# Attend and feed-forward parts of a Performer block as one program: the crossing between them written out per engine

## The reference

```
out = x + attn(xn) + ffn(xn)

attn:  q,k,v = xn @ wq, wk, wv              (reshaped to B=4, S=2048; 16 heads of 32)
       phi(u) = exp(u@omega.T - |u|^2/2 - max) / sqrt(128) + 1e-6     (128 features)
       kv = sum_s phi(k) v ;  z = sum_s phi(k)
       a  = (phi(q) @ kv) / (phi(q) @ z) @ wo
       x1 = layernorm(xn + a)
       x2 = layernorm(x1 + gelu(x1 @ w1 + b1) @ w2 + b2)      (512 -> 2048 -> 512)
ffn:   xr, xk = mixes of xn and the row before it
       r  = sigmoid(xr @ W_r.T) * (relu(xk @ W_k.T)^2 @ W_v.T)
```

## Time and profile before

| | us |
|---|---|
| median of 3 runs | 3691.76 (3691.68 to 3693.3) |
| profiled execution | 3692.05 |
| its span in the trace | 3690.2 |
| PE busy | 3544.2 |
| DVE / ACT / POOL busy | 2070.7 / 1839.5 / 1394.2 |

### The profile page before, as it was taken

The page is one execution under the profiler, slowest core; times in us unless marked ns, Lnnn a source line. Parts: engine busy times, 40 slices in busy tenths (PEclk is TensorE's granted clock), DMA queues, the critical chain, the costliest instruction groups (busy, mean ns, idle before and its releaser), DMA issues. The chain is left out here.

```text
span 3690.2 us, 71667 instructions
## 1 busy us (share of the span) xinstructions
PE 3544.2 (96%) x27762; PEld 3105.4 (84%) x27762; DVE 2070.7 (56%) x3304; ACT 1839.5 (50%) x3976; POOL 1394.2 (38%) x957
## 2 busy tenths in 40 slices
PE   7999999999699999999999949999999999999998
PEld 6888888887588888888888849988889989888887
DVE  5877777777567777777777633333333333333332
ACT  5777777777456656565665633333333323333332
POOL 2554545454244545454454412222222222222222
PEclk9999999999799999999999979999999999999999
DMA  2222222221223232232323241111111111111111
GB/s 104 87 78 70 90 78 73 73 88 54 95 81 102 82 97 91 88 97 88 102 84 98 83 129 68 46 44 43 45 44 46 45 38 46 44 43 45 45 45 46
DMA packets 151680, 262.70 MB, mean 71 GB/s; under 512 B 23184, under 2 KB 44176, under 8 KB 151440
## 3 DMA queue, kind: packets, MB, share of 16 engines
q1 hardware_dynamic: 151440, 259.46, 20.9%
HBM read 155.48 MB, written 103.94 MB: 70 GB/s over the span
## 5 line engine op out<-in xcount | busy, mean ns | idle before, releaser
L1484 DVE TENSOR_TENSOR ffn_hT_lo<-ffn_hid,ffn_hT_hi 128x512 fp32r<-128x512 f32 x256 | 334.3, 1334 | 489.4 <-ACT ffn_hT_hi L1460 489.4
L97 PE MATMUL ffn_hidden<-ffn_yT_hi,ffn_wa_hi 128*128 128x256 f32 x2048 | 573.3, 280 | 11.8 <-DVE ffn_yT_lo L1480 11.8
L97 PE MATMUL ffn_hidden<-ffn_yT_hi,ffn_wa_lo 128*128 128x256 f32 x2048 | 573.3, 280 | 0.0
L97 PE MATMUL ffn_hidden<-ffn_yT_lo,ffn_wa_hi 128*128 128x256 f32 x2048 | 572.3, 279 | 0.0
L1451 ACT ACTIVATE ffn_hid<-ffn_hidden,ffn_bias 128x256 f32<-128x256 f32 x512 | 213.2, 467 | 669.6 <-PE ffn_hidden L97 650.8
L233 POOL TENSOR_TENSOR ffn_n_rstd<-ffn_n_base,ffn_n_power 128x2 f32<-128x2 f32 x32 | 22.4, 700 | 1073.7 <-DVE ffn_n_negmean L228 1073.7
L97 PE MATMUL ffn_result<-ffn_wb_hi,ffn_hT_hi 128*128 128x512 f32 x1024 | 412.2, 403 | 2.6 <-DVE ffn_hT_lo L1484 2.6
L97 PE MATMUL ffn_result<-ffn_wb_hi,ffn_hT_lo 128*128 128x512 f32 x1024 | 404.5, 395 | 0.0
L97 PE MATMUL ffn_result<-ffn_wb_lo,ffn_hT_hi 128*128 128x512 f32 x1024 | 404.2, 395 | 0.0
L97 PEld LDWEIGHTS ffn_hidden<-ffn_yT_hi,ffn_wa_hi 128*128 128x128 f32 x2048 | 384.5, 188 | 20.8 <-DVE ffn_yT_lo L1480 12.1
L97 PEld LDWEIGHTS ffn_hidden<-ffn_yT_lo,ffn_wa_hi 128*128 128x128 f32 x2048 | 385.0, 188 | 8.8
(11 more groups left out here) (238 smaller groups left out, 9876.8 us busy)
## 6 DMA issues: line engine op xcount, KB each, us to landing
attend_uq<-u_d SPq DMA_DIRECT2D x33, 512.0 KB, 4.6
ffn_y_in<-y_d SPq DMA_DIRECT2D x33, 512.0 KB, 3.6
keys_xin<-in_L_attn_x_dram SPq DMA_DIRECT2D x32, 512.0 KB, 5.3
xn_d<-keys_xn SPq DMA_DIRECT2D x32, 512.0 KB, 4.2
xT_d<-keys_xT_whole SPq DMA_DIRECT2D x32, 512.0 KB, 2.6
u_d<-keys_uq SPq DMA_DIRECT2D x32, 512.0 KB, 2.8
attend_xTf<-xT_d SPq DMA_DIRECT2D x32, 512.0 KB, 5.1
r_d<-attend_gate SPq DMA_DIRECT2D x32, 512.0 KB, 3.2
```

The source lines that it names most:

```text
L97: last = pe.matmul(out, stationary[a], moving[b], start=start and n == 0, stop=stop and n == len(TERMS) - 1)
L1484: dve.tensor_tensor(hT[n % HB].lo[:, :, :], hid[n % 2][:, :, :], f32(hT[n % HB].hi[:, :, :]), ALU.subtract).then_inc(h_ready[n % HB], 1)
```

## The change

Attend and feed-forward become one Block, with no barrier between them and one end for both.

- Tiles get addresses by hand. The attend tiles are laid out in a table. Most feed-forward tiles lie over attend tiles: the weights, cut in eight pairs each (wa0 to wa7, wb0 to wb7), over attend weights and buffers that die at different times; stages s, x_in, r_in over diff, mixed, xTf; y_in over uq; hT over ka, act_k2 and gate. PSUM banks are shared: result 0 is turn, hidden 0 to 3 are feat 0 to 3, result 1 is num, turn 0 and 1 are gated 0 and 1.
- In place of the barrier stand waits on attend's semaphores (`left`) at the first use of each place.
- The last attend group (-1 in the lists), the tails of the two before it, and feed-forward group 0 are one list per engine (`..._CROSSING`). On PE, after num 3 of the last group: turn, w1 0 to 2, w2 0 and 1, w1 3, then the last two wo, then the rest of group 0.
- Groups 1 to 31 of feed-forward are written out in Python, the hardware loop is gone. The loads of a group that doesn't exist (the old `after`) are gone, and so is the second identity.

```diff
+FFN_OVER = (("wa0_hi", "wk_hi", 0), ("wa0_lo", "wk_hi", 4096), ("wb0_hi", "wk_hi", 8192), ("wb0_lo", "wk_hi", 12288),
+            ("wa1_hi", "wr_hi", 0), ("wa1_lo", "wr_hi", 4096), ("wb1_hi", "wr_hi", 8192), ("wb1_lo", "wr_hi", 12288),
...
         def run(eng, do):
-            do("weights", 0, 0)
-            do("weights", 1, 0)
-            do("turn", 0, 0)
-            for job, n, lead in BODY:
-                if job == "w1" and n + 2 < NH:
-                    do("weights", n + 2, 0)
-                if job != "base":
-                    do(job, n, lead)
-                if job == "w1" and n == NH - 1:
-                    do("base", 0, 0)
-            with eng.Fori(1, G - 1) as g:
+            for g in range(1, G):
                 for job, n, lead in BODY:
-                    do(job, n, g + lead)
-            for job, n, lead in BODY:
-                if lead == 0:
-                    do(job, n, G - 1)
-
-        block = ctx.enter_context(nc.Block())
-
-        @block.sync
-        def _(sp):
-            sp.dma_start(y[:, :, :], y_g[0]).then_inc(y_loaded, 16)
-
+                    if g + lead < G:
+                        do(job, n, g + lead)
+
+        def room(n):
+
+            return ((left.k_full, G), (left.r_full, G), (left.r_full, G), (left.out_full, G), (left.num_full, NC * G),
+                    (left.num_full, NC * G), (left.wo_full, G), (left.wo_full, G))[n]
...
+                if job == "y" and g == 0:
+                    sp.wait_ge(left.q_turned, 2 * G)
+                    sp.wait_ge(left.squared, TG * G)
+                    sp.wait_ge(left.y_stored, 16)
+                    sp.dma_start(y[:, :, :], y_g[0]).then_inc(y_loaded, 16)
                 if job == "weights":
+                    if n == 0:
+                        sp.wait_ge(left.mix_full, 2 * G)
+                        sp.wait_ge(left.mix_ready, 2 * G)
+                        sp.wait_ge(left.carried, G + 1)
                     for k in (2 * n, 2 * n + 1):
                         wait(sp, w_split, k - ns + 1)
                         sp.dma_start(stage(k), pieces[k][0]).then_inc(loaded[k % ns], 16)
...
-                    sp.dma_start(y[:, :, :], y_g[after(g, G)]).then_inc(y_loaded, 16)
+                    if isinstance(g, int) and g == 0:
+                        sp.wait_ge(left.y_stored, 16 * G)
+                        sp.wait_ge(left.r_stored, 16 * G)
+                    if not (isinstance(g, int) and g == G - 1):
+                        sp.dma_start(y[:, :, :], y_g[g + 1]).then_inc(y_loaded, 16)
...
+                    if isinstance(g, int) and g == 0:
+                        pool.wait_ge(consts_loaded, 16 * 4)
+                        pool.wait_ge(left.sq_ready, TG * G)
+                        pool.wait_ge(left.feat_full[HC - 1], 4 * G)
...
+                    act.wait_ge(*room(n))
+                    if n == NH - 1:
+                        act.wait_ge(left.o_ready, 2 * G)
...
+                        if isinstance(g, int) and g < 2:
+                            pe.wait_ge(left.wo_free[m], G - 1 + g)
+                            pe.wait_ge(left.out_free[m], G)
...
+PE_CROSSING = (("attend", "max", 0, -1), ("attend", "num", 3, -2), ("attend", "k", 0, -1), ("attend", "max", 1, -1),
+               ("attend", "k", 1, -1), ("attend", "r", 0, -1), ("attend", "below", 0, -1), ("attend", "feat", 0, -1),
+               ("attend", "r", 1, -1), ("attend", "out", 0, -1), ("attend", "num", 0, -1), ("attend", "out", 1, -1),
+               ("attend", "feat", 1, -1), ("attend", "num", 1, -1), ("attend", "wo", 0, -2), ("attend", "num", 2, -1),
+               ("attend", "wo", 1, -2), ("attend", "num", 3, -1), ("ffn", "turn", 0, 0), ("ffn", "w1", 0, 0),
+               ("ffn", "w1", 1, 0), ("ffn", "w1", 2, 0), ("ffn", "w2", 0, 0), ("ffn", "w2", 1, 0),
+               ("ffn", "w1", 3, 0), ("attend", "wo", 0, -1), ("attend", "wo", 1, -1), ("ffn", "w1", 4, 0),
+               ("ffn", "w2", 2, 0), ("ffn", "w2", 3, 0), ("ffn", "w1", 5, 0), ("ffn", "w2", 4, 0),
+               ("ffn", "w1", 6, 0), ("ffn", "w1", 7, 0), ("ffn", "w2", 5, 0), ("ffn", "turn", 0, 1),
+               ("ffn", "w2", 6, 0), ("ffn", "w2", 7, 0))
+DVE_CROSSING = (("attend", "top", 0, -1), ("attend", "top", 1, -1), ("attend", "recip", 0, -2),
+                ("attend", "below", 0, -1), ("attend", "exp", 0, -1), ("attend", "o", 0, -2),
+                ("attend", "out", 0, -1), ("attend", "out", 1, -1), ("attend", "hi", 1, -1), ("attend", "wo", 0, -2),
+                ("ffn", "weights", 0, 0), ("attend", "wo", 1, -2), ("attend", "stats", 0, -2), ("ffn", "turn", 0, 0),
+                ("ffn", "weights", 1, 0), ("attend", "recip", 0, -1), ("ffn", "weights", 2, 0), ("ffn", "w1", 0, 0),
+                ("ffn", "w1", 1, 0), ("attend", "o", 0, -1), ("ffn", "weights", 3, 0), ("ffn", "weights", 4, 0),
+                ("attend", "wo", 0, -1), ("ffn", "w1", 2, 0), ("attend", "wo", 1, -1), ("ffn", "w1", 3, 0),
+                ("attend", "stats", 0, -1), ("ffn", "weights", 5, 0), ("ffn", "w1", 4, 0), ("ffn", "weights", 6, 0),
+                ("ffn", "weights", 7, 0), ("ffn", "w1", 5, 0), ("ffn", "w1", 6, 0), ("ffn", "w1", 7, 0),
+                ("ffn", "base", 0, 0), ("ffn", "turn", 0, 1), ("ffn", "end", 0, 0))
+ACT_CROSSING = (("attend", "num", 3, -2), ("attend", "norm", 0, -3), ("attend", "k", 0, -1), ("attend", "k", 1, -1),
+                ("attend", "r", 0, -1), ("attend", "below", 0, -1), ("attend", "exp", 0, -1), ("attend", "r", 1, -1),
+                ("attend", "num", 0, -1), ("attend", "oT", 0, -2), ("attend", "exp", 1, -1), ("attend", "hi", 1, -1),
+                ("attend", "num", 1, -1), ("ffn", "weights", 0, 0), ("attend", "num", 2, -1),
+                ("attend", "num", 3, -1), ("ffn", "turn", 0, 0), ("ffn", "weights", 1, 0), ("ffn", "weights", 2, 0),
+                ("attend", "norm", 0, -2), ("ffn", "w1", 0, 0), ("ffn", "w1", 1, 0), ("ffn", "weights", 3, 0),
+                ("attend", "oT", 0, -1), ("ffn", "weights", 4, 0), ("ffn", "w1", 2, 0), ("ffn", "w1", 3, 0),
+                ("ffn", "weights", 5, 0), ("ffn", "w1", 4, 0), ("attend", "norm", 0, -1), ("ffn", "weights", 6, 0),
+                ("ffn", "w1", 5, 0), ("ffn", "weights", 7, 0), ("ffn", "w1", 6, 0), ("ffn", "w1", 7, 0),
+                ("ffn", "turn", 0, 1), ("ffn", "end", 0, 0))
+POOL_CROSSING = (("attend", "norm", 0, -3), ("attend", "k", 0, -1), ("attend", "k", 1, -1), ("attend", "oT", 0, -2),
+                 ("attend", "stats", 0, -2), ("attend", "norm", 0, -2), ("attend", "oT", 0, -1),
+                 ("ffn", "base", 0, 0), ("attend", "stats", 0, -1), ("attend", "norm", 0, -1), ("ffn", "end", 0, 0))
+SP_CROSSING = (("attend", "den_store", 0, -2), ("attend", "xb", 0, -2), ("attend", "den_load", 0, -2),
+               ("attend", "rden_store", 0, -2), ("attend", "rep_load", 0, -2), ("ffn", "weights", 0, 0),
+               ("attend", "store_y", 0, -3), ("attend", "store_r", 0, -1), ("ffn", "y", 0, 0),
+               ("ffn", "weights", 1, 0), ("attend", "den_store", 0, -1), ("ffn", "weights", 2, 0),
+               ("attend", "den_load", 0, -1), ("attend", "xb", 0, -1), ("attend", "rden_store", 0, -1),
+               ("ffn", "weights", 3, 0), ("attend", "rep_load", 0, -1), ("ffn", "weights", 4, 0),
+               ("attend", "store_y", 0, -2), ("ffn", "weights", 5, 0), ("ffn", "weights", 6, 0),
+               ("ffn", "weights", 7, 0), ("attend", "store_y", 0, -1), ("ffn", "base", 0, 0), ("ffn", "end", 0, 0))
...
+        @block.tensor
+        def _(pe):
+            attend_do, ffn_do = attend.tensor(pe), ffn.tensor(pe)
+            crossing(pe, attend_do, ffn_do, PE_CROSSING)
+            ffn_run(pe, ffn_do)
+
+    end_of(nc, attend.scope, ffn.scope)
 
```

More of the change, by code:

```diff
@@ L1285, in feed_forward_pass @@
     HB = 4
-    mem = Scope(nc, "ffn_")
+    mem = Scope(nc, "ffn_", places)
     ctx = ExitStack()
@@ L1436, in do @@
                 if job == "turn":
+                    if isinstance(g, int) and g == 0:
+                        for j in range(HC):
+                            act.wait_ge(left.feat_full[j], 4 * G)
                     for m in range(HB):
@@ new lines, in performer_and_gated_block, with crossing @@
+    ffn_places, end = lay_out(end, *FFN_ALONE)
+    for name, over, at in FFN_OVER:
+        ffn_places[name] = places[over] + at
+    ffn, ffn_run, y_loaded, stored = feed_forward_pass(
+        nc, ffn_places, left, ident, x_rows, w1, b1, w2, b2, ln2_g, ln2_b, y_d, r_d, out_rows, n_groups)
+    def crossing(eng, attend_do, ffn_do, order):
+        for where, job, n, g in order:
+            if where == "attend":
+                attend_do(job, n, n_groups + g, B - 1, S // GT + g)
+            else:
+                ffn_do(job, n, g)
```

190 lines of the change are left out of this document (120 added, 70 removed), and 10 rows, old and new, of tables (ATTEND, FFN_OVER).

## The result

The changed kernel took 3630.08 us (median of 4 runs, 3627.76 to 3632.11), the kernel before 3691.72 beside it (3685.24 to 3693.3): ratio 0.9838, 95% interval [0.9822, 0.9853], a gain of 61.6 us. I had said 3645, range 3636 to 3657. The direction was right, the time lies 15 us under the forecast and 6 us under the range. The profiled execution took 3627.76 us, its span is 3625.6.

What follows compares the result with a forecast made beforehand. PE, busy 96% of the span, bounds the kernel, so only its idle or half-clock time can be won. 46.3 - 3.5 + 4.1 = 46.9 us saved gives 3645 us, range 3636 to 3657.

Steps and rivals of the forecast that it cites:

- The crossing: Between attend and feed-forward: overlaying heads and tails saves 52.9 us less 6.5 of holes and 0.1, so 46.3 us.
- rival D: Denominator loads queue behind weights on SP or PE's new waits bind; 17.3 of 46.9 us lost, 3662 us; chance 0.07.
- Group 1's first w1: Sign in the changed profile: feed-forward group 1 begins its first w1 at 2191.7 to 2195.
- Gap a: PE idles 1.8 us before w1 0, having no other job while ACT and DVE copy and split the turned y.
- Gap b: PE idles 1.8 us before w1 2, waiting for the fifth weight piece, whose split ends on DVE at 2142.6.
- Gap c: PE idles 2.9 us before w2 0, its gelu standing behind rounding, a norm and a table load on ACT.
- w1 3: Its seventh weight piece is split directly after o at 2153.2, PE asks at 2154.0: 0.8 us spare only.
- Clock: Holes within the crossing lower PE's granted clock for one episode: 3.5 us lost, bounds 0 and 10.
- Rival C: Weights starve PE: some 5 splits meet POOL, 6 us, or the clock stays low; say 3655 us; chance 0.20.
- The loop written out: Feed-forward groups 1 to 30: about 0.5 us more slack per group for the r load, 4.1 us saved, bounds 0 and 6.4.
- Rival E: Slower than before: PE waits for fetching written-out feed-forward code; at 2 us per group 3705 us; chance 0.03.
- At nothing. Placing the tensors by hand: Giving tiles hand-written addresses was counted at no gain or loss, like dropping the second identity and cutting the weights.

Runs made afterwards that it cites:

- the three kernels of the last set: Changed kernel unaltered, 3629.8 us; with ka and hT at 128 bytes, 3614.55 us; with operands back at old places but for ka, 3643.53 us.

## Why the prediction was right and wrong, point by point

**The crossing (right).** Forecast 46.3 less 3.5 for the clock, 42.8; measured 43.4, and 42.4 with the operands at their old places (96.4 us for the stretch, before 138.8), so the placing doesn't flatter it. The rival D (cover of oT fails) didn't come: 0.3 us remains of 17.3. Group 1's first w1 came at 2182.96, 9 us ahead of the 2191.7 to 2195 that I had named; attend's start and its norms, 11.4 us together, had already moved it. The single gaps were less right than their sum. DVE's timeline of the kernel after shows why:

```profile
2131.20 0.35 DVE L1170 RECIPROCAL attend_rden<-attend_den 128x32 f32<-128x32 f32 x1 [5.05 <-DMA attend_den<-den_d]
2131.47 1.16 DVE L1525 TENSOR_TENSOR ffn_wa_lo<-ffn_x_in,ffn_wa_hi 128x1024 fp32r<-128x1024 f32 x1
...
2136.35 3.39 DVE L1534 TENSOR_TENSOR ffn_hT_lo<-ffn_hid,ffn_hT_hi 128x512 fp32r<-128x512 f32 x2 [2.58 <-ACT ffn_hT_hi L1511]
2141.28 2.47 DVE L1174 TENSOR_TENSOR attend_o<-attend_raw,attend_o 64x1024 f32<-64x1024 f32 x2 [1.54 <-DMA attend_o<-rden_d]
2143.78 1.23 DVE L1525 TENSOR_TENSOR ffn_wa_lo<-ffn_s,ffn_wa_hi 128x1024 fp32r<-128x1024 f32 x1
...
2146.06 3.42 DVE L1525 TENSOR_TENSOR ffn_wa_lo<-ffn_r_in,ffn_wa_hi 128x1024 fp32r<-128x1024 f32 x1
...
2162.22 2.14 DVE L1525 TENSOR_TENSOR ffn_wa_lo<-ffn_s,ffn_wa_hi 128x1024 fp32r<-128x1024 f32 x1 [1.99 <-ACT ffn_wa_hi L1478]
```

- Gap a: 1.7 for 1.8.
- Gap b: 3.1 for 1.8. The fifth piece was rounded by ACT at 2126.69, but its split stands behind the reciprocal on DVE, and the denominators came 1.4 us later than I put them. The order on DVE's queue, which I had named, set it, not the piece.
- Gap c: 1.1 for 2.9. The excess that I charged beside POOL was 1.2, where half of o's is 1.04. hT_lo was ready 0.9 us after my time, but PE was later itself, by gap b and the clock.
- w1 3, for which I counted 0.8 us to spare, waited 1.1, behind `o`. I had the replicated denominators 3 us too early.
- Clock: w1 2 took 4.26 us where the two before it took 2.9 each, 1.3 lost, in windows of 0.92 and 0.74; I had 3.5 from the earlier trace rows. In a second profile of the same program the dip (0.66) came 5 us later, over w2 0 and w2 1, and cost 7.2 - 5.6 = 1.6 us.
- Rival C, the weights starve PE. What it lived on came, and PE did not starve. The Trainium skill ("SBUF — State Buffer", Who interferes with whom) has a VectorE instruction with two SBUF inputs and a GpSimd instruction that reads SBUF exclude each other; the trace agrees here too: hT_lo took 3.39 for two beside POOL's norm. Of the 16 splits of weights, 12 took 1.16 to 1.23, as alone. Where one of these met an operation of POOL, it was POOL's that got longer (at 2132.87 2.04 against 1.27 for a later one alike, at 2144.92 oT_lo 3.49 against 2.40 before). The other four took 3.42 and 2.58 beside POOL's oT_lo and yb, and 2.14 and 2.31 beside its last norm, 5.5 us more than alone; in the kernel before all 16 took 1.21 to 1.23. The estimate in C was five splits and 6 us. But they are the 9th, 10th, 13th and 14th, and in PE's waits no piece behind the 7th appears: they had the slack that I had counted for w1 4 to w1 7.

**The loop written out (not borne out by the time).** I had read 0.5 us of slack off SP's issue of the r load after POOL's yb. It is there:

```profile
2978.26 2.89 POOL L1454 TENSOR_TENSOR ffn_yb<-ffn_y_in,ffn_bias 128x1024 f32<-128x1024 f32 x1
```

```profile
2982.21 0.47 SPq L1436 DMA_DIRECT2D ffn_r_in<-r_d  x1
```

The issue comes 2982.21 - (2978.26 + 2.89) = 1.06 us after yb's end, where it was 1.57. But alone the edit measured 1.0003, at most 2.6 us. The losses that the slack was to remove are still there: in the changed kernel the load of r stays on the chain, and the periods exceed their floor by 3.6 us in one profile and 8.5 in the next, which is also the scatter that the 6.4 us of the kernel before belong to. I had taken the scatter of one profile for a cost that an edit can remove. What the edit did take off in the traces is something that I had not seen, 0.09 us of the floor (2.7 in 30 groups). This was tried in one set of runs, the one with the kernel before at its fastest (3684.82). In the two sets where it had 3699.55 and 3700.67, no other kernel with the loop ran; whether the loop costs more there was not tested. Rival E (code fetch) didn't come: 3.65 MB of instructions instead of 2.54, and PE waits for none.

**"At nothing. Placing the tensors by hand" (the step that failed).** It is worth 13.7 us in the changed kernel (the one with the old places against the changed kernel beside it, 4 runs each, no overlap). In their traces 5.7 of them lie in attend (1039.4 against 1033.7 from the 1st to the 30th norm), 30 x (46.03 - 45.88) = 4.5 in the feed-forward floor, and 2.2 in the crossing; the rest is within the scatter of single periods. The sentence in the prediction had no row behind it and no bound, and without this term the range, worked out with care from the holes, missed: 3630.08 + 13.7 = 3643.8 would lie in it. The chain in the earlier trace rows gave a hint: 24 products in 2.83 us are 118 ns each, and nobody had asked why not less. The Trainium skill ("SBUF — State Buffer", Who interferes with whom) gives TensorE two independent read ports, for the moving operand and for the weight load, that no other engine shares. Taken to the letter, a place would cost nothing, and the sum would be mine. The sweeps differ with that reading, 116.5 to 119.9 and 228.5 to 233.7 ns by place alone, and the measurement decides.

**The start (luck), and what the miss of 15 us is made of.** 5.7 us of the profiled difference lie ahead of attend, and all of them are within what unchanged code does from run to run. The medians, not the profiles, carry the result; by them the forecast missed by 15 us. The placing is 13.7 of it, but that the two nearly agree is partly chance. I had also counted 4.1 for the loop where the time shows at most 2.6, so between 3 and 5.5 us of the gain have no term, about what an early or a late start is worth. And the gain itself isn't one number: the kernel before had medians from 3684.8 to 3699.6 (once 3700.7) in the sets of runs, while the changed kernel had 3630.1 and 3629.8, so the gain was 61.6 in the first set and 69.8 in the last. No trace of the kernel before was taken where it was slow, and why it differs is open. The differences between the three kernels of the last set, 13.7 and 15.2, don't hang on it.

**What stays open.** Why a place matters. The spacing by yT's place repeats with 256 bytes (16 places over 512 bytes); for hT eight places within 256 were tried. Which reads or writes meet there isn't shown by any row. Nor is it known whether the moving and the stationary place count each alone or by their distance, since the weights stayed at 128 in all runs. In attend the moving mix at 224 and at 128 gave k the same 121.6 to 121.9 ns in the mean, so w1's differences between places don't hold for all products. Single distances did change: they spread from 114 to 124 ns at 224, and at 128 most of them are 120. The keys pass was the same in all kernels and served as control (28.21 or 28.22 us a group in each).

## What to carry to other kernels

Where PE is busy over 95%, read the distance of its products from start to start before and after, by shape, and treat a change of any tensor's address as a term of the sum, with a bound: here it moved a job of 24 products between 2.80 and 2.88 us and one of 12 between 2.75 and 2.80. Sweep the place group by group within one run; two such runs gave what five single kernels didn't, and 256 bytes of padding then won 15 us. Compare two kernels only within one set of runs, for the kernel before moved by 15 us from set to set. A hole in a hand-written order is set by what stands ahead on the queue that is late, so moving a job that is ahead of another hole only moves the hole.

## What the runs showed of the hardware

- The time of a matmul depends on where its operands lie, by the address modulo 256 bytes: 256-column fp32r products 116.5 to 119.9 ns apart by the moving operand's place, 512-column ones 228.5 to 233.7 by the stationary's, and 228.9 in the kernel with ka and hT at 128.
- The granted clock in the window 45 to 55 us differs between executions of one program (1.00 and 0.66), and the start of attend with it (1053.2 and 1056.6). Over 15 traces of kernels with the same code there it is 1.00, 0.83 or 0.66, and attend starts at 1053.0 to 1058.9.
- Writing out a loop of 30 groups (2.54 to 3.65 MB of instructions) did not change the time: 1.0003 [0.9993, 1.0012]. In the traces a group's period is 0.09 us shorter (46.12 to 46.03).
- A split of weights on DVE (two SBUF inputs) took 1.16 to 1.23 us alone and up to 3.42 beside an operation of POOL.
